# One graph layer's edge rows through a DRAM table, and the next layer's VectorE operands in PSUM

## The reference, cut to what matters

```python
# layer 0, shapes: h [3125,128], he [100000,64]
h = x @ node_fc_W + node_fc_b;  hs, hd = h[src], h[dst]
alpha = seg_softmax(sum(hs * hd, -1), dst)            # per destination node
g = sigmoid(relu(he @ rel_att_W1 + b1) . rel_att_W2 + b2);  beta = seg_softmax(g, dst)
h_att = segment_sum(alpha * (hs @ node_att_W), dst) / 3
h_rel = segment_sum(sum_m beta[m] * (hs @ rel_att_W[m]), dst) / 3
h_red = relu(concat(h_att, h_rel) @ out_fc_W + out_fc_b)
out = gate * where(deg > 0, h_red, h) + (1 - gate) * x
# layer 1, segments now by src
q, k = (X @ Wq)[src], (X @ Wk)[dst];  e = tanh(q + k)
p = exp(e @ Wphi - max);  alpha = p / (segment_sum(p, src)[src] + 1e-9)
out = segment_sum(alpha * ((X @ Wy_w + b)[dst] + e @ We), src)
```

## Time and profile before

| what | value |
|---|---|
| time, median of 3 runs | 2787.11 us (2782.03 to 2795.92) |
| time of the profiled execution | 2772.86 us |
| its span, first to last instruction | 2771.2 us |
| mean granted TensorE clock, share of full speed | 0.898 |
| busy: PE, DVE, ACT, POOL | 78%, 66%, 55%, 61% |
| DMA packets and bytes | 211670, 290.63 MB |
| first edge pass | about 637 to 1499 us, 293 steps |
| second edge pass | about 1651 to 2699 us, 220 steps |

### The profile page before, as it was taken

How to read it: one execution, slowest core, us unless ns; L and a number is a source line. 1 busy time by engine, 2 the same in 40 slices (tenths; PEclk the granted TensorE clock), 3 DMA queues, 4 the chain that set the end, 5 groups by cost and what they waited for, 6 DMA issues and landing times. The chain is left out here.

```text
span 2771.2 us, 64649 instructions
## 1 busy us (share of the span) xinstructions
PE 2167.7 (78%) x16604; PEld 1454.2 (52%) x16604; DVE 1815.4 (66%) x6215; ACT 1528.7 (55%) x4445; POOL 1687.2 (61%) x1772
## 2 busy tenths in 40 slices
PE   6799999996888888888888376776777777777773
PEld 4333333334666666666667345555555555555552
DVE  8965464105666666766666637777778777777764
ACT  2466766774555555555554115555555555555541
POOL 1377777765555565556552017777777777777750
PEclk9999999997999999999999658889888889888985
DMA  9244444544444444444443012222222222222220
GB/s 97 72 137 130 134 134 145 143 114 133 152 153 154 156 149 150 155 149 151 156 149 104 5 43 76 74 75 74 74 76 77 75 73 74 77 77 75 76 53 24
DMA packets 211670, 290.63 MB, mean 105 GB/s; under 512 B 87104, under 2 KB 136149, under 8 KB 211568
## 3 DMA queue, kind: packets, MB, share of 16 engines
q0 software_dynamic: 76160, 172.95, 23.0%
q1 hardware_dynamic: 135408, 116.54, 14.1%
HBM read 183.24 MB, written 28.70 MB: 76 GB/s over the span
## 5 line engine op out<-in xcount | busy, mean ns | idle before, releaser
L1575 POOL DMA_INDIRECT sum_acc<-kv_table,rec_all x784 | 790.0, 1008 | 239.2 <-issue 229.9
L1079 POOL DMA_INDIRECT area_b<-h_table,src_g x448 | 454.6, 1015 | 339.9 <-issue 184.7
L514 POOL DMA_INDIRECT early<-h_table,src_g x336 | 331.2, 986 | 222.0 <-ACT sum_acc L729 142.0
L729 ACT ACTIVATE sum_acc<-twin,bias 128x1024 f32<-128x1024 f32 x294 | 317.9, 1117 | 155.1 <-PE twin L599 151.3
L1661 ACT COPY sum_acc<-sum_acc 128x768 f32 x220 | 183.4, 834 | 378.0 <-POOLq L1581 290.4
L1176 ACT COPY y_sb<-bank 128x512 f32<-128x512 f32 x293 | 171.5, 585 | 329.4 <-PE bank L1140 327.7
L1149 PE MATMUL bank<-hs,y_sb 128*128 128x129 f32 x2344 | 323.6, 282 | 0.7 <-ACT y_sb L1172 0.6
L599 PE MATMUL twin<-area_b,wc 64*128 64x512 f32 x1176 | 313.5, 634 | 10.9 <-ACT sum_acc L729 10.9
L1140 PE MATMUL bank<-identf,hs 128*128 128x128 f32 x1172 | 196.2, 292 | 138.9 <-DMA hs<-area_b 137.2
L1149 PEld LDWEIGHTS bank<-hs,y_sb 128*128 128x128 f32 x2344 | 296.8, 198 | 5.1 <-issue 3.8
L1267 DVE SCALAR_TENSOR_TENSOR sum_acc<-sum_acc,shrink,bank 128x129 f32 x293 | 102.2, 349 | 277.0 <-ACT m_old L1193 172.6
(11 more groups left out here) (311 smaller groups left out, 4540.1 us busy)
## 6 DMA issues: line engine op xcount, KB each, us to landing
hs<-area_b SPq DMA_DIRECT2D x293, 258.0 KB, 2.4
area_b<-in_edge_attr SPq DMA_DIRECT2D x97, 256.0 KB, 2.9
rows_table<-early POOLq DMA_DIRECT2D x84, 258.0 KB, 3.0
area_b<-rows_table POOLq DMA_DIRECT2D x84, 258.0 KB
sum_acc<-kv_table,rec_all POOLq DMA_INDIRECT x784
area_b<-h_table,src_g POOLq DMA_INDIRECT x448
early<-h_table,src_g POOLq DMA_INDIRECT x336
kv_table<-sum_acc SPq DMA_DIRECT2D x25, 96.0 KB, 1.6
```

The costliest lines, as they stand in the source:

```text
L514: pool.indirect_dma_start(out=early[:, g % RINGE, j, 0:D], out_offset=None, in_=h_table, in_offset=bass.IndirectOffsetOnAxis(ap=src_g[:, e ...
L729: act.activation(hid_words[:, first:first + 2 * GE], twin[p % 2][:, :], ACT.Relu, bias=bias1[:, m:m + 1]).then_inc(hid_sb, 1)
L1079: pool.indirect_dma_start(out=landed_rows[:, k * GT + j, 0:D], out_offset=None, in_=h_table, in_offset=bass.IndirectOffsetOnAxis(ap=src_g[ ...
L1575: pool.indirect_dma_start(out=landed_rows[:, g % RING1 * GT + j, :], out_offset=None, in_=kv_table, in_offset=bass.IndirectOffsetOnAxis(ap ...
```

## The change

Layer 0: `rows_table` now has a place for each of the 196 groups. The preparation fills the places of groups 0 to 83, no longer of a spread selection. In the first pass GpSimd gathers groups 84 to 195 into a ring of 4 SBUF buffers and stores each in `rows_table`. It raises `ready` by 84 at the start and by one as each store has landed. It no longer waits for `stepped`. SyncE's load of each step reads `rows_table` in DRAM instead of the SBUF ring, so `plan_s` needs no ring place. `fetch` and the ring of 16 are gone.

Layer 1: in the second pass VectorE's operands `iota_n` and `phi_b` are copied once into PSUM bank 6, `pen` lies in bank 6, and `p_e`, written by ScalarE, in bank 7.

```diff
-EARLY_GROUPS = [g for g in range(GROUPS) if g * EARLY % GROUPS < EARLY]
-        rows_table = dram("rows_table", [EARLY, 128, GT * (D + 1)])
+        rows_table = dram("rows_table", [GROUPS, 128, GT * (D + 1)])
@@ preparation, GpSimd
-                    for g, early_group in enumerate(EARLY_GROUPS):
+                    for g in range(EARLY):
...
@@ first pass
-            landed_rows = area_b[:, 0:RING0 * GT * (D + 1)].rearrange("p (e d) -> p e d", d=D + 1)
+            landed_rows = area_b[:, 0:RINGE * GT * (D + 1)].rearrange("p (e d) -> p e d", d=D + 1)
@@ SyncE, load(s, k)
-                        at = sp.value_load(plan_s[0:1, bass.ds(n, 1), 1], min_val=0, max_val=(RING0 - 1) * GT)
                         sp.wait_ge(stepped, n + SU0 - SH + 1)
                         sp.wait_ge(ready, groups)
                         sp.dma_start(hs[:, k, :, :].rearrange("p j d -> p (j d)"),
-                                     landed_rows[:, bass.ds(at, GT), :].rearrange("p j d -> p (j d)")).then_inc(step_in[k], 16)
+                                     rows_table[bass.ds(within(groups - 1, GROUPS - 1), 1), :, :].rearrange("o p c -> (o p) c")).then_inc(step_in[k], 16)
@@ GpSimd
+                    def store(g):
+                        pool.wait_ge(early_in[g % RINGE], 64 * (g // RINGE + 1))
+                        pool.sem_inc(ticks, 1)
+                        pool.dma_start(rows_table[g, :, :],
+                                       landed_rows[:, g % RINGE * GT:(g % RINGE + 1) * GT, :].rearrange("p j d -> p (j d)")).then_inc(early_out[g % RINGE], 16)
                     def arrived(g):
-                        pool.wait_ge(landed[g % 4], sum(16 if n in EARLY_GROUPS else 64 for n in range(g % 4, g + 1, 4)))
+                        pool.wait_ge(early_out[g % RINGE], 16 * (g // RINGE + 1))
                         pool.sem_inc(ready, 1)
-                    for g in range(GROUPS):
-                        if g >= RING0:
-                            last_step = pool.value_load(reach_row[0:1, g - RING0:g - RING0 + 1], min_val=0, max_val=STEPS0 - 1)
-                            pool.wait_ge(stepped, last_step + SU0 + 1)
-                        if g in EARLY_GROUPS:
-                            fetch(g, g % RING0)
-                        else:
-                            gather(g, g % RING0)
-                        if g > 1:
-                            arrived(g - 1)
-                        if g == 0:
-                            arrived(0)
+                    pool.sem_inc(ready, EARLY)
+                    for g in range(EARLY, GROUPS):
+                        gather(g)
+                        if g >= EARLY + 2:
+                            arrived(g - 2)
+                        if g > EARLY:
+                            store(g - 1)
+                    arrived(GROUPS - 2)
+                    store(GROUPS - 1)
                     arrived(GROUPS - 1)
@@ second pass
-            pen = sb4("pen", [128, RING, GT])
-            p_e = sb4("p_e", [128, 2, GT])
+            iota_ps = bank[6][:, 0:BN]
+            phi_ps = bank[6][:, BN:BN + AD]
+            pen = bank[6][:, 256:256 + RING * GT].rearrange("p (u j) -> p u j", u=RING)
+            p_e = bank[7][:, 0:2 * GT].rearrange("p (q j) -> p q j", q=2)
...
+                    v.tensor_copy(iota_ps, iota_n[:, :]).then_inc(cleared_v, 1)
+                    v.tensor_copy(phi_ps, phi_b[:, :]).then_inc(cleared_v, 1)
...
-                        v.tensor_tensor(onehot_v[:, k % RING, :, :], iota_n[:, :].unsqueeze(1).to_broadcast([128, GT, BN]),
+                        v.tensor_tensor(onehot_v[:, k % RING, :, :], iota_ps.unsqueeze(1).to_broadcast([128, GT, BN]),
...
                         v.tensor_tensor(prod[:, :, :], row_v[:, k % RING, :, KV:KV + AD],
-                                        phi_b[:, :].unsqueeze(1).to_broadcast([128, GT, AD]), ALU.mult).then_inc(prod_done, 1)
+                                        phi_ps.unsqueeze(1).to_broadcast([128, GT, AD]), ALU.mult).then_inc(prod_done, 1)
```

More of the change, by code:

```diff
@@ L36 @@
 PAIRS0 = GROUPS + WINS - 1
-RING0 = 16
 EARLY = 84
 RINGE = 4
-EARLY_GROUPS = [g for g in range(GROUPS) if g * EARLY % GROUPS < EARLY]
 ROUNDS0 = STEPS0 + 8
@@ L67 @@
 FAR = -1e6
-assert len(EARLY_GROUPS) == EARLY and EARLY_GROUPS[0] == 0 and EARLY % RINGE == 0
+assert EARLY % RINGE == 0
 assert GROUPS % 2 == 0 and GH <= 128 and W == 5 and NB % W == 0
@@ L116, in build @@
         plan_v = sb("plan_v", [1, ROUNDS0, 4], I32)
-        plan_s = sb("plan_s", [1, STEPS0, 2], I32)
+        plan_s = sb("plan_s", [1, STEPS0], I32)
         plan_l = sb("plan_l", [1, STEPS], I32)
@@ L927, in _ @@
                     step(v.tensor_scalar(reset0[:, :], reset0[:, :], NO_EDGE, None, ALU.mult))
-                    step(v.tensor_scalar(plan_s[:, :, 0], row_g, 1.0, None, ALU.add))
-                    step(v.tensor_scalar(plan_s[:, :, 1], row_g, RING0 - 1, None, ALU.bitwise_and))
-                    step(v.tensor_scalar(plan_s[:, :, 1], plan_s[:, :, 1], float(GT), None, ALU.mult))
+                    step(v.tensor_scalar(plan_s[:, :], row_g, 1.0, None, ALU.add))
                     step(v.tensor_scalar(at(plan_v, 6, 3), row_b, float(WN), None, ALU.mult))
@@ L1017, in build @@
             HALF = WALL // 2
-            landed = [sem2(f"landed0_{k}") for k in range(4)]
             ready = sem2("ready0")
@@ L1053, in load @@
                         n = s * SU0 + k
-                        groups = sp.value_load(plan_s[0:1, bass.ds(n, 1), 0], min_val=1, max_val=GROUPS)
-                        at = sp.value_load(plan_s[0:1, bass.ds(n, 1), 1], min_val=0, max_val=(RING0 - 1) * GT)
+                        groups = sp.value_load(plan_s[0:1, bass.ds(n, 1)], min_val=1, max_val=GROUPS)
                         sp.wait_ge(stepped, n + SU0 - SH + 1)
@@ L1070, in _, with gather @@
                 def _(pool):
-                    def fetch(g, k):
-                        pool.sem_inc(ticks, 1)
-                        pool.dma_start(landed_rows[:, k * GT:(k + 1) * GT, :].rearrange("p j d -> p (j d)"),
-                                       rows_table[EARLY_GROUPS.index(g), :, :]).then_inc(landed[g % 4], 16)
-                    def gather(g, k):
+                    def gather(g):
                         pool.sem_inc(ticks, 1)
@@ L1079, in gather @@
                             pool.indirect_dma_start(
[L1080 to L1081 removed]
+                                out=landed_rows[:, g % RINGE * GT + j, 0:D], out_offset=None, in_=h_table,
+                                in_offset=bass.IndirectOffsetOnAxis(ap=src_g[:, g * GT + j:g * GT + j + 1], axis=0)).then_inc(early_in[g % RINGE], 16)
+                    def store(g):
[3 more added lines that the diff above has]
+                                       landed_rows[:, g % RINGE * GT:(g % RINGE + 1) * GT, :].rearrange("p j d -> p (j d)")).then_inc(early_out[g % RINGE], 16)
                     def arrived(g):
[L1084 removed]
+                        pool.wait_ge(early_out[g % RINGE], 16 * (g // RINGE + 1))
                         pool.sem_inc(ready, 1)
                     pool.wait_ge(cleared, 5)
[L1088 to L1099 removed]
+                    pool.sem_inc(ready, EARLY)
[7 more added lines that the diff above has]
+                    store(GROUPS - 1)
                     arrived(GROUPS - 1)
@@ L1594, in _ @@
                     pe.wait_ge(cleared, 3)
-                    pe.wait_ge(cleared_v, 5)
+                    pe.wait_ge(cleared_v, 7)
                     def turn(s, k):
@@ L1652, in _ @@
                     act.wait_ge(cleared, 3)
-                    act.wait_ge(cleared_v, 5)
+                    act.wait_ge(cleared_v, 7)
                     def move_rows(s, k, at):
```

6 lines of the change are left out of this document (2 added, 4 removed).

## The result

The changed kernel takes 2567.39 us (median of four runs, 2566.85 to 2568.50), the kernel before 2788.61 us (median of four, 2782.03 to 2795.92). The ratio is 0.9207, with a 95% interval of 0.9183 to 0.923: 221 us less. Forecast were 2605 us, so 182 less. The profiled execution of the changed kernel took 2568.5 us, its span is 2566.9 us.

A forecast was written before the change was run, and what follows sets the result against it. The prediction saw the first pass bound by GpSimd and TensorE waiting on each other, the second by GpSimd's gathers. Gains of 140 + 42 = 182 us took 2787 to 2605 us, range 2560 to 2680, the forecast's own 2585 to 2635.

The forecast's parts named there:

- The first pass: 140 us forecast: First pass: TensorE no longer waits for late rows, gaining 140 us, between 125 and 159.
- the 20 us: First pass: about 20 us lost to TensorE's clock dropping to 1.2 GHz, of which a part was expected back.
- The 2.6 us counted for the start: Start of the first pass: one load replaces fetch and copy, saving 2.6 us.
- rival 4: TensorE's clock never falls back in the first pass, 159 us come whole, with 49 in the second: 2579 us; chance 0.12.
- GpSimd 5.9 us a group: First pass: GpSimd needs 5.9 us for each later group's four gathers and store, with all gathered at 1298 us.
- Lead 38 us: First pass: GpSimd is 38 us early for TensorE at the tightest point.
- the last landing waited for: End of the first pass: the last group's store was counted to land in 3.1 us.
- A load 0.71 us of the DMA engines: First pass: each DRAM load takes 0.71 us of all 16 DMA engines, total share 61%; upper bound 2.1 us.
- Second pass: 42 us forecast: Second pass: gathers shorten with operands in PSUM, gaining 42 us, between 20 and 49.
- the step of 4.46 us: Second pass: if all the gathers' excess goes, GpSimd needs 980 us, 4.46 us a step.
- VectorE's instructions cost the same: Second pass: a PSUM operand leaves VectorE's instruction time unchanged, 424 ns against 426 from SBUF.
- Rival 3: First pass: loads from DRAM bound it, making the kernel slower, 2915 us at 3.5 us a load; chance 0.05 with other losses.

The follow-up runs named there:

- e1: The changed kernel with the second pass's operands iota_n, phi_b, pen and p_e back in SBUF: 2627.66 us, ratio 0.9437 to the kernel before.
- e3: The kernel before, SBUF ring kept, with GpSimd reporting group g-2 instead of g-1 after issuing group g: 2648.66 us, ratio 0.9521.
- e4: The changed kernel with 72 groups stored in the preparation instead of 84: 2610.31 us, ratio 0.9384 to the kernel before.
- e11: The changed kernel with every step's load from DRAM issued twice, on a slow chip: 3630.40 us, ratio 1.0391 to the kernel before there.
- e2: The kernel before with only the second pass's operands moved to PSUM: 2714.94 us, ratio 0.9767.
- e5: The changed kernel with iota_n alone in PSUM, on a slow chip: 3561.89 us, ratio 1.0217 to the kernel before there.
- e6: The changed kernel with p_e alone in PSUM, on a slow chip: 3612.99 us, ratio 1.0369 to the kernel before there.
- e12: The changed kernel with the zeroing of acc_st moved from GpSimd to VectorE, on a slow chip: 3629.06 us, ratio 1.0394 to the kernel before there.
- e13: The kernel before, unchanged, traced on a slow chip: 3506.82 us in one run.

## Why the prediction was right, and where it was off

- *The first pass: 140 us forecast, 153 in the profiles, 156 by e1.* The cause was the one named: `ready` was late because GpSimd waited behind each fetch and gather, and with that gone TensorE never waits. e3 shows it by itself. The term was too small by the clock: "a part" of the 20 us was counted back, and all came (1.00). The 2.6 us counted for the start did not come: the wait before the first step fell by 1.2 us and the pass began 0.7 us earlier. The 2.35 us a step and the end of filling gave 702 us where 700 was the lower bound. That is rival 4's first half.
- *GpSimd 5.9 us a group, all gathered at 1298 us*: 5.90 and 1299. *Lead 38 us*: 24 to 28 by e4. The pass ended 12 us sooner than counted (1344 against 1356) and the last landing waited for took 5.2 us, not 3.1, which makes 24.
- *A load 0.71 us of the DMA engines, share 61%*: 0.95 us and 74%, within the bounds of 0.71 to 2.1, but a third above the value taken. Rows from DRAM beside gathers cost more than SBUF copies did. Nothing waited for it, and e11 gives room to twice as many once no gathers run.
- *Second pass: 42 us forecast, 49 in the profiles, 60 by e1, 69 by e2.* The cause was the one named: gathers that start inside L1726, L1756 and L1769 were the long ones, and none is now. The excess over the median went completely, and the step of 4.46 us came; neither TensorE nor VectorE took over, for which 7 us had been taken off. The term was also mis-sized for another reason: the excess was read from one profiled execution, faster than all four runs of the result. In others it is 60 to 67 us (e1, e3). That is likely the 14 us between that execution and the median too, which the sum carried over to the kernel after, whose runs lie within 1.7 us of each other. The forecast was 38 us too high: 13 are the first pass, 7 the second in the profiles, 17 that the medians differ by 221 us where the profiles differ by 204. The time lies inside the range of 2560 to 2680 us, but below the forecast's own 2585 to 2635 and 12 us below rival 4's 2579: of the cases put down, rival 4's both halves came, with the 17 us on top.
- The rule of the Trainium skill weighed in the prediction ("SBUF — State Buffer", Who interferes with whom), that VectorE with two SBUF inputs contends with GpSimd reading SBUF, agrees with e1 and e2, 1023 ns against 946, and with e5 and e6 instruction by instruction. The same section's sentence that `tensor_tensor` was not seen to stall a DMA does not hold for the issue of these indirect gathers.
- *VectorE's instructions cost the same*: 692 ns against 697, 417 against 426; ScalarE's `p_e` 267 against 297, a small gain that lay beside GpSimd.
- *Rival 3, slower*, was wrong here in its mechanism. But on two other chips the kernels with this change that gather without a pause are slower than before (e12, the changed kernel but for one zeroing, by 3.9%), by another mechanism that I had not among the rivals and that the trace before does not show. The change itself, unedited, ran on no such chip.

## What to carry to other kernels

If an engine issues transfers and also announces that they have landed, let it announce the group before last: moving one wait by one group gained 135 of 2784 us here, with nothing else changed. Where GpSimd's gathers bound a stage, look at their mean against their median; if they differ, give each VectorE instruction beside them that reads two tensors one of them in PSUM, and take the price from several executions, not from one profile. On the chips of e5 to e13 the operands in PSUM did not shorten the pass, since GpSimd waited for the others there. Time a kernel that lets one engine issue without a pause on more than one chip before calling it faster.

## What the runs showed of the hardware

- The kernel before takes 2784 us on one chip and 3480 us on three others; the stages with gathers are long there (1162 us against 855, and 1395 against 1028, in e13), the preparation less so (687 against 643). A change that gains 8% on the one kind (0.9207) goes with a loss of 4% on the other (e12, 1.0394).
- On those chips what ScalarE and VectorE wait for from TensorE comes late while GpSimd issues gathers back to back (medians of 16 to 27 us of waiting, one copy 47 us after its matmuls, e12); what TensorE waits for from them does not (0.15 us at most in the median). The granted clock is 0.50 in these stretches, with TensorE busy 18 of 200 us.
- A gather that starts inside a VectorE instruction on two tensors in SBUF is longer: 1138 ns in the mean in L1726 (128x512), 1113 in L1769, 1035 in L1756 (128x256), against 946 with one of the two in PSUM (before and after). The means over all gathers differ from execution to execution: 1008, 1023, 1032 and 1017 ns; with the operands in PSUM 945 to 947 ns in all traces.
- ScalarE's write of 128x4 to PSUM took 267 ns, to SBUF 297.
- A 258 KB store to DRAM landed 2.4 to 5.4 us after its issue in the preparation, 3.0 in the median (trace before).
